# Scaling of queries and keys in two halves, with a signal after each

## The reference

```python
q, k = l2norm(q) * qs, l2norm(k) * ksc                 # over the 64 numbers of each head
q = q * cos * scale + rotate_half(q) * sin * scale
k = k * cos * inv + rotate_half(k) * sin * inv
out = local_attention(q, k, v)                         # windows of 32 tokens, and the window before
```

## Time and profile before

| | |
|---|---|
| median of 3 runs | 5669.12 us (5667.3 to 5673.87) |
| the profiled execution | 5667.65 us, its span 5665.8 us |
| PE, PEld busy | 4785.3 us (84%), 3219.6 us (57%) |
| DVE, ACT, POOL busy | 4254.1 us (75%), 3789.1 us (67%), 2480.3 us (44%) |
| granted TensorE clock, mean | 0.962 |

### The profile page before, as it was taken

One profiled execution on the slowest core, in us unless ns is written; L12 is line 12 of the kernel. 1 busy time (PEld: TensorE's weight loads), 2 busy tenths in 40 slices (PEclk: granted clock), 3 DMA queues, 4 the chain that ended last, 5 costly groups with the idle time before them and its releaser, 6 DMA issues.

```text
span 5665.8 us, 133229 instructions
## 1 busy us (share of the span) xinstructions
PE 4785.3 (84%) x47928; PEld 3219.6 (57%) x48122; DVE 4254.1 (75%) x6024; ACT 3789.1 (67%) x7196; POOL 2480.3 (44%) x1142
## 2 busy tenths in 40 slices
PE   3349999999958888888888888888888888888886
PEld 1124478888835555555555555555555555555554
DVE  6761155566678888888888888888888888888886
ACT  3323255555547777777777777777777777777775
POOL 0100000000046565665656656565665656566564
PEclk7669999999979999999999999999999999999998
DMA  2000000000010000000000000000000000000001
GB/s 59 0 0 0 0 20 0 0 0 0 0 39 0 0 0 0 19 0 0 0 0 19 0 0 0 4 15 0 0 0 19 0 0 0 0 19 0 0 0 34
DMA packets 43314, 34.86 MB, mean 6 GB/s; under 512 B 3771, under 2 KB 39062, under 8 KB 42262
## 3 DMA queue, kind: packets, MB, share of 16 engines
q1 hardware_dynamic: 43286, 34.52, 2.0%
HBM read 30.32 MB, written 4.19 MB: 6 GB/s over the span
## 4 chain that ended last, share of the span: by engine, by line
PE 44%; DVE 22%; issue 16%; ACT 9%; DVEq 2%; ACTq 0%; POOL 0%; DMA 0%; SPq 0%; POOLq 0%
DVE arena L927 6%; PE bank L1356 5%; PE bank L1446 5%; PE bank L802 4%; PE bank L766 4%; DVE arena L948 4%; PE bank L534 4%; DVE arena L955 4%; PE bank L1404 4%; PE bank L1382 4%; ACT arena L1174 3%; PE bank L753 2%; PE bank L757 2%; PE bank L787 2%; DVE arena L965 2%
## 5 line engine op out<-in xcount | busy, mean ns | idle before, releaser
L1298 POOL TENSOR_TENSOR arena<-arena,rope_d 128x512 f32<-128x512 f32 x780 | 1296.2, 1693 | 1000.3 <-DVE arena L936 1000.3
L1304 POOL TENSOR_TENSOR arena<-arena 128x2048 f32<-128x2048 f32 x195 | 898.8, 4609 | 424.5 <-DVE arena L948 407.4
L1404 PE MATMUL bank<-m_vo,arena 128*32 128x512 f32 x6144 | 743.8, 603 | 171.0 <-ACT arena L1174 168.5
L948 DVE TENSOR_TENSOR arena<-arena,rope_d 128x1024 f32<-128x1024 f32 x390 | 728.9, 1889 | 13.4
L1356 PE MATMUL bank<-wqk_split,x_split 128*128 (+1 forms) x2352 | 670.9, 421 | 15.9 <-ACT arena L1122 11.0
L1122 ACT ACTIVATE arena<-bank 128x512 f32<-128x512 f32 x784 | 453.3, 598 | 324.8 <-PE bank L1356 303.3
L1280 POOL TENSOR_TENSOR rope_d<-rope,qk_scale 128x128 f32 (+1 forms) x14 | 6.4, 457 | 1228.7 <-DVE x_all L1022 1228.7
L1366 PE MATMUL bank<-ident,arena 128*128 128x128 f32 x3104 | 435.8, 284 | 120.6 <-ACT arena L1145 65.0
L1404 PEld LDWEIGHTS bank<-m_vo,arena 128*32 128x32 f32 x6144 | 160.3, 109 | 621.8 <-ACT arena L1174 484.6
L1356 PEld LDWEIGHTS bank<-wqk_split,x_split 128*128 128x128 f32 x2352 | 430.4, 190 | 134.6 <-issue 19.7
L927 DVE TENSOR_REDUCE arena<-arena 128x16 f32<-128x1024 f32 x390 | 455.4, 1209 | 7.7 <-ACT arena L1129 7.7
(11 more groups left out here) (228 smaller groups left out, 9327.2 us busy)
## 6 DMA issues: line engine op xcount, KB each, us to landing
wqk_stage<-in_wqk SPq DMA_DIRECT2D x8, 1024.0 KB, 6.9
out_x<-x_all SPq DMA_DIRECT2D x8, 512.0 KB, 5.4
wvt<-in_wvt SPq DMA_DIRECT2D x7, 512.0 KB, 4.0
wo<-in_wo SPq DMA_DIRECT2D x7, 512.0 KB, 5.2
w<-in_w SPq DMA_DIRECT2D x7, 341.0 KB
arena<-in_wbh SPq DMA_DIRECT2D x1, 2048.0 KB, 9.9
arena<-out_x SPq DMA_DIRECT2D x4, 512.0 KB, 5.8
w<-in_w SPq DMA_DIRECT2D x7, 128.0 KB
```

The costliest lines, as they stand in the source:

```text
L948: nc.vector.tensor_tensor(d_rot[j][:, m * H:(m + 1) * H, :], d_raw[j][:, m * H:(m + 1) * H, :], tab, ALU.mult)\
L1298: last = nc.gpsimd.tensor_tensor(d_t2[:, m * H:(m + 1) * H, a:a + half], d_raw[j][:, m * H:(m + 1) * H, z:z + half], rope_d[:, bass.ds(par ...
L1304: nc.gpsimd.tensor_tensor(d_rot[j], d_rot[j], d_t2, ALU.add).then_inc(s_rope, 1)
L1404: last = nc.tensor.matmul(bank[6 + w % 2][q * WIN:(q + 1) * WIN, :], d_xv[:, w * WIN:(w + 1) * WIN], m_vo[:, 4 * q:4 * q + 4, :].rearrange ...
```

## The change

The scaling of L936 becomes a loop over the two halves, queries and keys, with a signal after each, and the counts of those who wait for `s_norm` follow: VectorE's cosine products and GpSimd's sine products wait for their own half.

```diff
-            nc.vector.tensor_tensor(d_raw[j], d_raw[j], d_y.unsqueeze(2).to_broadcast([P, 2 * H, DH]), ALU.mult)\
-                .then_inc(s_norm, 1)
+            for m in range(2):
+                heads = slice(m * H, (m + 1) * H)
+                nc.vector.tensor_tensor(d_raw[j][:, heads, :], d_raw[j][:, heads, :],
+                                        d_y[:, heads].unsqueeze(2).to_broadcast([P, H, DH]), ALU.mult).then_inc(s_norm, 1)
 
         def front_cos(dve, f, j, halves=(0, 1)):
 
             par = layer_of(f) & 1
-            dve.wait_ge(s_norm, TPS * f + j + 1)
             dve.wait_ge(s_tab, layer_of(f) + 1)
             if not (isinstance(f, int) and f == 0):
                 dve.wait_ge(s_tp, slot_of(f - 2, QK[j]) + 4)
             for m in halves:
+                dve.wait_ge(s_norm, 2 * (TPS * f + j) + m + 1)
                 tab = rope_d[:, bass.ds(par, 1), j, m, :].to_broadcast([P, H, DH])
@@ rotate
                 at_least(pool, s_rope, i)
-                pool.wait_ge(s_norm, i + 1)
                 for m in range(2):
+                    pool.wait_ge(s_norm, 2 * i + m + 1)
                     for a, z in ((0, half), (half, 0)):
```

## The result

The changed kernel takes 5758.74 us at the median of 4 runs (5756.51 to 5763.61), the kernel before 5670.28 us beside it: a ratio of 1.0158, 95% interval 1.0144 to 1.0173. It is slower, as forecast, but by 88.5 us instead of 37. The measured time lies within the stated range by a microsecond, and that is luck: the range's bounds hold nothing of the term that was missing.

What follows compares the result with a forecast made beforehand. Bound by a chain mostly of TensorE and VectorE, with VectorE and GpSimd alternating on one resource. Terms -35.5 + 97 - 24.6 = +36.9 us on 5667.65, plus 1.5 to the median: 5706 us; range 5634 to 5760.

Steps and rivals of the forecast that it cites:

- The first tile gains 0.37 us a pass, 35.5 us.: At j=0, GpSimd's first product and the sums L927 come 0.37 us earlier in each of 96 passes: -35.5 us.
- the prediction's other estimate: Split price on VectorE from the skill's N+151 cycles: two halves cost 0.16 us more than the whole scaling.
- The second tile costs 1.01 us a pass through the copy, 97 us.: At j=1, GpSimd's waiting product delays token copy L911, then L1341 and L1113, by 1.01 us a pass: +97 us.
- The feed-forward norm gives 24.6 us back.: L991 goes in short ahead of GpSimd's fourth product every time, ending TensorE's wait for L994: -24.6 us.
- From there everything to L955 moves.: After L1113 and L1190, all work to the pass's end shifts with the late copy: 96 x 1.01, +97 us.
- the bounds -19 and +110 us for the tiles: Forecast limits over 96 passes: first tile gaining only 0.2 us a pass, second tile costing 1.15.
- the norm's own bounds: Limits for L991's effect: -24.6 us, or +20 if all the other 46 passes got the long form.
- The first rival: At j=1, VectorE keeps the resource or the copy precedes the product; only the first tile's gain: 5637 us, chance 0.20.
- The second (GpSimd gets in at the first tile): At j=0, GpSimd's product runs between the halves, second L948 ends 1.14 us later: 5850 us, chance 0.10.
- The third (nothing that can be told): Both tiles' effects meet unseen slack, leaving the split's price, +4 us: 5673 us, chance 0.10.

Runs made afterwards that it cites:

- first tile, copy ahead: Against the kernel before: only the j=0 scaling split and signalled by halves, and VectorE's token copy L911 put ahead of the j=1 scaling; 5668.2 us.
- first tile only: Against the kernel before: only the scaling of j=0 split and signalled by halves, j=1 keeping one operation and one signal; 5668.1 us.
- halves, one wait: Against the changed kernel: scaling still in halves, but GpSimd waits for both before its first sine product; 5672.3 us.
- second tile only: Against the kernel before: only the scaling of j=1 split and signalled by halves; 5856.1 us.

## Why the prediction was right and wrong

The steps against what was measured, in the prediction's order:

1. *The first tile gains 0.37 us a pass, 35.5 us.* Right. GpSimd's first product ended 0.32 us earlier against the scaling; clean passes went from 40.68 to 40.35; with the clock up it is worth 37.2 us. The split cost 0.07 us (2.36 for 2.29), not 0.04, and well under the 0.16 of the prediction's other estimate.
2. *The second tile costs 1.01 us a pass through the copy, 97 us.* Right in every joint. Three durations measured as they had been written down beforehand (forecast in brackets): the second half 1.75 us (1.75), L1316 1.36 (1.5), L911 1.34 (1.35). TensorE's idle time ahead of the transposes grew by 1.03 us. With the clock up the second tile measured 94.9 us.
3. *The feed-forward norm gives 24.6 us back.* Right in the main. TensorE's wait for L994 fell from 24.6 us to 6.4:

```profile
L993 DVE SCALAR_TENSOR_TENSOR arena<-arena x97: 424/1300/2922, 1677.1 to 5723.5; 128x256 f32<-128x256 f32 x97
...
  PE bank L1448: 6.4, 5
```

That is 18 us. The forecast that L991 would be short nearly everywhere missed: it was long in 48 passes, 41 of them at half clock.

4. *"From there everything to L955 moves."* This is the step that failed. It took the 1.01 us by which TensorE stands idle longer as the whole price, with TensorE's work behind it as long as before: the clock stood in the sum at nothing, without a reason. It was at half in 53 passes instead of 12. The traces' passes add up, over the 95 intervals, with the two kinds of longer pass counted by what they last beyond a clean one with a short L991: the length of a clean pass with a short L991, 40.68 to 41.40 us, over the 90 passes that aren't at a layer's end, +65 (forecast 0.64 us a pass, measured 0.72); clean passes with a long L991, 44 to 7, -18; passes with a stretch at half clock, 7 to 48, +36; the 5 passes at the layers' ends +8; the rest -2. That is 89 of the 89.8 us. So the sum lacked 36 us for the clock, and some more at the layers' ends. The runs with TensorE kept busy agree: the transposes give the changed kernel 62.5 us (5758.7 to 5696.2) and the kernel before 22.7 (5670.3 to 5647.6), 40 us apart, of which the norm's L991 is a part.

The way through the copy and the sign were right, and the size was off by more than a factor of two, because one mechanism was missing. The range's top, 5760, is the sum of the bounds -19 and +110 us for the tiles, and leaves out the +20 us that the norm's own bounds allowed. The first rival (VectorE keeps the resource) fell by the rows of j = 1, at a joint that went as the one between two L948 in the earlier trace rows. The second (GpSimd gets in at the first tile) fell by the rows of j = 0, where the second half started at once, as in the pair L927. The third (nothing that can be told) fell by the time.

That the clock is a part of the sum could have been read before: of the 12 passes of the kernel before that had a stretch at half clock, 4 had it from 1.8 us behind the copy's start, behind 1.4 us of idle TensorE, and 3 more, each just behind a layer's end, from 3.1 to 3.6 us behind it. The Trainium skill (TensorE: Matmul & The Clock Gate, "Part 1: The HAM clock gate") says that the array's clock is at half by default and that activity releases it. That would have put a price on idle TensorE time beyond its length, and the runs with TensorE kept busy agree: 12 to 92 passes with a stretch at half clock became 5.

What stays open is what makes the clock fall in one pass and not in its neighbour, which has the same idle time (2.46 and 2.47 us above). That the idle time of TensorE lets it fall is shown by filling it. That a longer idle time in front of the transposes makes it fall more often is not shown; the kernels don't follow that order:

| kernel | idle TensorE in front of the transposes, median, us | passes with a stretch at half clock |
|---|---|---|
| first tile, copy ahead | 0.33 (1.31 more just behind them) | 46 |
| before | 1.40 | 12 |
| first tile only | 1.42 | 38 |
| halves, one wait | 2.44 | 26 |
| changed | 2.46 | 53 |
| second tile only | 3.50 | 92 |

The passes of these kernels also differ in length (40.35 us with the first tile alone, 40.68 or 41.11 before). That this decides it was not tried.

## What to carry to other kernels

An earlier signal lets the other engine stand in line earlier, and where two engines take turns on one resource its next instruction goes ahead of yours: ask of every instruction behind a split who waits for it, and split only where nobody on the chain does (here the first tile and not the second, and even that paid only with TensorE's wait filled). When a change makes TensorE wait longer in front of dense work, price the wait and the clock apart, and try a few needless transposes in the wait: here eight of them took 22.7 us off the kernel before and 57.7 off the one with the first tile split.

## What the runs showed of the hardware

- Eight needless transposes, one every 0.11 us, in a wait took 22.7 us off a kernel that is otherwise the same (part of it through the feed-forward norm), and 57.7 us off the one with the first tile split; passes with a stretch at half clock went from 12 and 38 to 5.
- Who goes first at the shared resource turned within 0.06 us, and went the same way in all 95 passes of a kernel: a cosine half ready 0.01 us ahead of the product ran bare in 1.22 us, one ready 0.05 us behind it took 2.32.
